# A four-batch WKV and FFN kernel on one core: `w` over ScalarE's queue, eight-column expert masks spread by a product, and another order on all engines

## What is computed

```python
decay = exp(-exp(w)) * (0.5 + 0.5 * tf)
# forward and backward scans  a = a * decay + x  over ek*v (numerator) and ek (denominator)
num = nf + nb - ekv + euk * vf
den = df + db - ek + euk
out = sigmoid(r) * (num / max(den, 1e-8)) * (0.8 + 0.2 * tf)

# layer 0: x = x + experts(WKV(x)): 8 experts of rank 64, one per token by the largest gate
gate = argmax(softmax(xf @ Wg.T)); h = (xf @ A.T) * one_hot(gate); y = h @ Bw.T * 4 * prob
# layer 1: x = x + FFN(WKV(x)): ternary weights made from w1 and w2, 1024 hidden, exact gelu
out = gelu(x @ q(w1).T + b1) @ q(w2).T + b2
```

## Time and profile before

| | |
|---|---|
| median of 3 runs | 103.1 us (101.97, 103.10, 103.27) |
| the profiled execution's own time | 102.21 us |
| its span, first to last instruction | 100.4 us |
| PE busy | 89.8 us, 89% |
| DVE busy | 86.5 us, 86% |
| ACT busy | 79.9 us, 80% |
| POOL busy | 66.3 us, 66% |
| granted TensorE clock, mean | 1.00 |
| HBM read, written | 5.26 MB, 1.05 MB |

### The profile page before, as it was taken

How to read it: one execution, slowest core, us unless ns; L and a number is a source line. 1 busy time by engine, 2 the same in 40 slices (tenths; PEclk the granted TensorE clock), 3 DMA queues, 4 the chain that set the end, 5 groups by cost and what they waited for, 6 DMA issues and landing times. The chain is left out here.

```text
span 100.4 us, 2070 instructions
## 1 busy us (share of the span) xinstructions
PE 89.8 (89%) x633; PEld 80.9 (81%) x633; DVE 86.5 (86%) x203; ACT 79.9 (80%) x144; POOL 66.3 (66%) x90
## 2 busy tenths in 40 slices
PE   3897669989978999999799999999899999799980
PEld 2686549977777888888588888889799999699970
DVE  2479999999999999999999999999999997983330
ACT  4279999999986769999766589997997899976520
POOL 4067679979985697059769897999982967005310
PEclk9999999999999999999999999999999999999999
DMA  1889999700000000000000000000000021100005
GB/s 20 258 262 320 308 245 378 313 3 0 3 0 0 3 0 7 0 0 0 0 3 0 7 0 0 0 0 0 0 0 7 0 104 70 35 0 10 0 0 209
DMA packets 6886, 6.43 MB, mean 64 GB/s; under 512 B 2370, under 2 KB 6492, under 8 KB 6876
## 3 DMA queue, kind: packets, MB, share of 16 engines
q1 hardware_dynamic: 6868, 6.31, 20.1%
q10 hardware_dynamic: 8, 0.00, 0.0%
HBM read 5.26 MB, written 1.05 MB: 63 GB/s over the span
## 5 line engine op out<-in xcount | busy, mean ns | idle before, releaser
L298 POOL TENSOR_TENSOR h_lo<-h,h_hi 128x512 fp32r<-128x512 f32 x9 | 12.3, 1373 | 12.0 <-DVE h_hi L306 7.0
L794 DVE TENSOR_TENSOR_SCAN run<-bank,kv 128x256 f32<-128x256 f32 x32 | 20.0, 670 | 0.1
L1224 PE MATMUL bank<-xin_hi,w1T 128*128 128x256 f32 x64 | 15.8, 287 | 0.9 <-DVE xin_lo L292 0.5
L1156 PE MATMUL bank<-num,AT 128*128 128x256 f32 x64 | 15.5, 384 | 0.7 <-DVE hm L900 0.5
L1258 PE MATMUL bank<-w2T,h_hi 128*128 128x256 f32 x64 | 16.1, 288 | 0.0
L1258 PE MATMUL bank<-w2T,h_lo 128*128 128x256 f32 x64 | 15.6, 281 | 0.0
L611 ACT ACTIVATE h<-bank,bT 128x256 f32<-128x256 f32 x32 | 13.3, 478 | 2.8 <-PE bank L1224 2.6
L1224 PE MATMUL bank<-xin_lo,w1T 128*128 128x256 f32 x64 | 15.2, 278 | 0.0
L1172 PE MATMUL bank<-hm,BT 128*128 128x256 f32 x64 | 14.6, 382 | 0.1
L1224 PEld LDWEIGHTS bank<-xin_hi,w1T 128*128 128x128 f32 x64 | 12.0, 188 | 1.8 <-DVE xin_lo L292 0.8
L1156 PEld LDWEIGHTS bank<-num,AT 128*128 128x128 f32 x64 | 11.6, 190 | 2.2 <-issue 0.9
(11 more groups left out here) (141 smaller groups left out, 216.5 us busy)
## 6 DMA issues: line engine op xcount, KB each, us to landing
w_nat<-in_L_ffn_w_dram SPq DMA_DIRECT2D x2, 1024.0 KB, 8.3
F_nat<-in_fside_BxSxS_dram SPq DMA_DIRECT2D x4, 256.0 KB, 3.5
x_nat<-in_x_dram SPq DMA_DIRECT2D x4, 256.0 KB, 4.9
out_dram<-outb SPq DMA_DIRECT2D x3, 256.0 KB, 2.1
A_nat<-in_L_ffn_A_dram SPq DMA_DIRECT2D x1, 512.0 KB, 5.8
...
wv_rows<-in_L_cond_w_dram SPq DMA_DIRECT2D x2, 1.0 KB
```

Of the source, the lines that this page charges most:

```text
L298: eng.tensor_tensor(h_lo[:, b % 2, 2 * j:2 * j + 2], h32[:, b % 2, 2 * j:2 * j + 2], h_hi[:, b % 2, 2 * j:2 * j + 2].bitcast(F32), ALU.sub ...
L794: dve.tensor_tensor_scan(run[:, r, c, q], decay_ps[:, l, c, b:b + 1].broadcast_to([P, T]), kv[:, b, c, q], 0.0, ALU.mult, ALU.add).then_in ...
L1156: mm = pe.matmul(bank[H_BANK + k][:, (m % 2) * T:(m % 2 + 1) * T], AT[:, c, m * P:(m + 1) * P], num_at(0, b)[:, c], start=(c == 0), stop=( ...
L1224: mm = pe.matmul(bank[g_bank[g]][:, (f % 2) * T:(f % 2 + 1) * T], w1T[:, c, f * P:(f + 1) * P], part[:, b % 2, c], start=(c == 0 and part ...
```

## The change

1. `w` is loaded from ScalarE's queue, and `exp(-exp(w))` is taken on the four rows before the transpose, not after it. VectorE reads the decay's factor from PSUM.
2. An expert mask has 8 columns, one per expert. TensorE transposes it to 8 rows, ScalarE copies these (`copy_hot`), and a product with the constant matrix `spread` (8x128, ones where the partition belongs to the expert) gives the 128 rows (`spread_mask`), which ScalarE copies as before.
3. The reciprocal of the gate's sum leaves `expert_mask` and becomes a call of its own, placed earlier.
4. All four call lists are in a new order, and some calls change engine. To GpSimd go `clip_keys(1)`, `times_tanh(2)` and `(3)`, `h_low(0,3)`, `(1,1)`, `(3,2)`. To VectorE go `seed(0,0,DEN)`, both `seed(1,2)`, `own_values(1,3)`, `add_num(1,2)`, `h_low(1,3)`, `(2,0)`, `(3,1)`, `h_high(1,3)`, `(2,1)`, `(3,2)`, `(3,3)`. To ScalarE go `h_high(2,0)`, `(2,2)`, `(2,3)`.
5. ScalarE has two table loads fewer (ten instead of twelve with the first). TensorE has 21 `keep_warm` transposes instead of 46 and 7 `warm_up` instead of 10.

```diff
-            for k, v in enumerate((w_l0, w_l1)):
-                sp.dma_start(wv_rows[NC * k:NC * (k + 1), :], v.rearrange("(c p) -> c p", p=P)).then_inc(wv_loaded, 16)
...
+            for k, v in enumerate((w_l0, w_l1)):
+                act.dma_start(wv_rows[NC * k:NC * (k + 1), :], v.rearrange("(c p) -> c p", p=P)).then_inc(wv_loaded, 16)
             act.preload_act_table_set("natural_log_exp_and_others")
 
             def decay_exps():
-                act.wait_ge(front_psum, 2)
-                act.activation(edecay[:, :], bank[MISC_BANK][:, VEC_AT:VEC_AT + LAYERS * NC], ACT.Exp).then_inc(edecay_ready, 1)
+                act.wait_ge(wv_loaded, 16 * LAYERS)
+                act.activation(wv_rows[:, :], wv_rows[:, :], ACT.Exp).then_inc(edecay_ready, 1)
                 act.wait_ge(edecay_ready, 1)
-                act.activation(edecay[:, :], edecay[:, :], ACT.Exp, scale=-1.0).then_inc(edecay_ready, 1)
+                act.activation(wv_rows[:, :], wv_rows[:, :], ACT.Exp, scale=-1.0).then_inc(edecay_ready, 1)
...
+            def copy_hot(b):
+                act.wait_ge(hot_psum, b + 1)
+                act.activation(hot_rows[:, b % 2], bank[MISC_BANK][0:NE, MASK_AT:MASK_AT + T], ACT.Copy).then_inc(hot_copied, 1)
...
-            def expert_mask(b):
-
+            def gate_reciprocal(b):
                 both = slice(NT * b, NT * (b + 1))
                 dve.wait_ge(gsum_ready, NT * (b + 1))
                 dve.reciprocal(bank[DVE_BANK][:, GREC_AT + NT * b:GREC_AT + NT * (b + 1)], gsum[:, both]).then_inc(grec_ready, 1)
+
+            def expert_mask(b):
+
...
-                    dve.tensor_scalar(mask[:, i % (2 * NT)], expert_ps, bank[DVE_BANK][:, IDX_AT + i:IDX_AT + i + 1],
+                    dve.tensor_scalar(hot[:, i % (2 * NT)], expert_ps, bank[DVE_BANK][:, IDX_AT + i:IDX_AT + i + 1],
...
-                    mm = pe.transpose(bank[MISC_BANK][:, MASK_AT + n * P:MASK_AT + (n + 1) * P], mask[:, NT * (b % 2) + n], ident[:, :])
-                mm.then_inc(mask_psum, 1)
+                    mm = pe.transpose(bank[MISC_BANK][0:NE, MASK_AT + n * P:MASK_AT + (n + 1) * P], hot[:, NT * (b % 2) + n], ident[:, :])
+                mm.then_inc(hot_psum, 1)
+
+            def spread_mask(b):
+                pe.wait_ge(hot_copied, b + 1)
+                pe.wait_ge(consts_ready, 7 + NE)
+                pe.matmul(bank[MISC_BANK][:, MASK_AT:MASK_AT + T], spread[:, :], hot_rows[:, b % 2], start=True, stop=True).then_inc(mask_psum, 1)
...
             hidden(0, 0)
             hidden(0, 1)
+            expert_in(3, 0)
             transpose_mask(3)
```

More of the change, by code:

```diff
@@ L418, in _ @@
             clip_first_keys(pool, 0)
+            gains()
             clip_first_keys(pool, 1)
-            gains()
             times_values(pool, 0)
             factors()
-            seed(pool, 0, 0, DEN)
-            seed(pool, 0, 1, DEN)
+            clip_keys(pool, 2)
+            clip_keys(pool, 1)
             seed(pool, 0, 0, NUM)
@@ L449, in _ @@
             own_values(pool, 1, 0)
-            add_one(0)
+            own_values(pool, 0, 3)
+            add_num(pool, 0, 3)
             seed(pool, 1, 0, NUM)
-            add_num(pool, 0, 3)
             times_sigmoid(pool, 3)
@@ L455, in _ @@
             num_times_rec(0, 3)
+            add_b2(0)
             add_num(pool, 1, 0)
+            add_one(0)
             times_tanh(pool, 0)
-            add_b2(0)
+            add_one(1)
             num_times_rec(1, 0)
             seed(pool, 1, 1, DEN)
+            seed(pool, 1, 1, NUM)
             add_b2(1)
+            xin_low(pool, 0)
             own_values(pool, 1, 1)
-            add_one(1)
-            xin_low(pool, 0)
-            own_values(pool, 1, 2)
-            seed(pool, 1, 1, NUM)
-            own_values(pool, 1, 3)
             add_num(pool, 1, 1)
             times_tanh(pool, 1)
-            h_low(pool, 0, 0)
-            seed(pool, 1, 2, DEN)
-            add_b2(2)
-            xin_low(pool, 1)
-            h_low(pool, 0, 1)
-            seed(pool, 1, 2, NUM)
-            add_one(2)
+            own_values(pool, 1, 2)
+            xin_low(pool, 1)
+            add_one(2)
+            add_b2(2)
+            h_low(pool, 0, 1)
+            h_low(pool, 0, 0)
             h_low(pool, 0, 2)
-            add_num(pool, 1, 2)
+            h_low(pool, 0, 3)
             h_low(pool, 1, 0)
+            times_tanh(pool, 2)
+            add_b2(3)
+            h_low(pool, 1, 1)
             h_low(pool, 1, 2)
-            h_low(pool, 1, 3)
             add_one(3)
-            h_low(pool, 2, 0)
-            add_b2(3)
-            h_low(pool, 3, 1)
+            times_tanh(pool, 3)
+            h_low(pool, 3, 2)
             h_low(pool, 3, 3)
@@ L627, in _ @@
             sigmoid(3)
+            evacuate_Wg()
             act.preload_act_table_set("natural_log_exp_and_others")
-            key_exp(2)
+            log_den(0, 0)
+            reciprocal(0, 0)
             evacuate_A(0)
@@ L913, in _ @@
             forward_chunk(0, 0, DEN, 0)
+            inverse_gains()
             forward_chunk(0, 0, DEN, 1)
-            clip_keys(dve, 1)
-            inverse_gains()
-            forward(0, 1, DEN)
+            seed(dve, 0, 0, DEN)
+            backward(0, 0, DEN)
+            place_factors()
             forward(0, 0, NUM)
-            place_factors()
-            backward(0, 0, DEN)
             own_keys(0, 0)
             backward(0, 0, NUM)
-            own_keys(0, 1)
+            forward(0, 1, DEN)
             add_den(0, 0)
@@ L985, in _ @@
+            product(1, 1)
+            xin_high(dve, 1)
+            forward(1, 2, DEN)
             select_expert(3, 0)
             select_expert(3, 1)
-            refine_rec(1, 1)
-            forward(1, 2, DEN)
-            product(1, 1)
-            xin_high(dve, 1)
+            seed(dve, 1, 2, DEN)
+            forward(1, 2, NUM)
             backward(1, 2, DEN)
             add_den(1, 2)
-            forward(1, 2, NUM)
+            forward(1, 3, NUM)
+            seed(dve, 1, 2, NUM)
+            own_values(dve, 1, 3)
@@ L994, in _ @@
+            backward(1, 2, NUM)
+            add_num(dve, 1, 2)
             forward(1, 3, DEN)
-            backward(1, 2, NUM)
             den_times_rec(1, 2)
-            forward(1, 3, NUM)
-            times_tanh(dve, 2)
+            refine_rec(1, 2)
             seed(dve, 1, 3, NUM)
             seed(dve, 1, 3, DEN)
-            refine_rec(1, 2)
             product(1, 2)
-            h_low(dve, 0, 3)
-            h_low(dve, 1, 1)
+            backward(1, 3, DEN)
             xin_low(dve, 2)
-            backward(1, 3, DEN)
+            add_den(1, 3)
@@ L1020, in _ @@
+            h_high(dve, 3, 0)
             h_low(dve, 2, 2)
-            h_high(dve, 3, 0)
             h_low(dve, 3, 0)
             h_high(dve, 3, 1)
-            h_low(dve, 3, 2)
-            h_low(dve, 2, 3)
+            h_high(dve, 3, 2)
+            h_low(dve, 3, 1)
+            h_high(dve, 3, 3)
             last_result(dve, 0)
```

289 lines of the change are left out of this document (152 added, 137 removed).

## The result

| | before | after |
|---|---|---|
| median | 103.1 us | 104.06 us (104.01 to 105.19, 5 runs) |
| ratio to the kernel before | | 1.0158, 95% interval 1.0096 to 1.0221 |
| the profiled execution's own time | 102.21 us | 105.19 us |
| its span | 100.4 us | 103.3 us |
| PE, DVE busy | 89.8, 86.5 us | 92.3, 87.1 us |

What follows compares the result with a forecast made beforehand. VectorE was taken to bound until expert_out(2), then TensorE's fixed work. Earlier start -2.0, more work +1.85, fewer waits -1.5 gave -1.65: 100.55 for the profiled execution, median 101.0 us, range 99.4 to 103.2.

Steps and rivals of the forecast that it cites:

- What bounds the kernel: Whole kernel: VectorE sets when layer 1's inputs appear; TensorE must then work off a fixed amount.
- TensorE's fixed work: From expert_out(2) to the last matmul: 41.9 us of work before, 43.75 after the change.
- the sum: From expert_out(2) to the last matmul after the change: 43.75 us of work and 1.1 of waits.
- the small things: On TensorE, four place_output, a mask, a residual and the last transpose_weights: estimated at 2.9 us.
- the waits: TensorE's waits and gaps after expert_out(2): 2.6 of 44.5 us, 1.1 of them left, a gain of 1.5.
- three signs of being wrong: VectorE idle beyond 1 us before 50 us, select_expert waiting for mask_rows, or slow transposes around 15 to 20 us.
- rival (3): Fewer keep_warm: TensorE falls to 1.2 GHz before gate_logits(0), layer 0's first 5.3 us double; 105.5 us; chance 0.06.
- 0.4 us on GpSimd: Delay on times_tanh(2) and (3), also delaying VectorE; part of a rival at 102.2 us, chance 0.20.
- The start: Program start to first scan: new path of w and fewer warm_up gain 0.2 us (bounds 0 and 0.8).
- The masks: On VectorE a mask takes 0.3 us instead of 0.93; three before select_expert(2,1) save 1.9.
- upper bound of 0.5: TensorE's added spread_mask(3) behind expert_out(2): 0.4 us, bounds 0.25 and 0.5.
- The slack of the mask: Between the end of batch 0's mask copy and its use: 1.5 us before, 0.75 in the new order.

Runs made afterwards that it cites:

- e9: Changed kernel with only own_values(1,3) and backward(1,2,NUM) swapped on VectorE: 102.96 us, ratio 1.0069.
- e14: As e11, with 19 and 27 keep_warm in place of 12 and 9: 101.83 us, ratio 0.9874.
- e4: Kernel before, in its old order, with the 8-column masks, copy_hot and spread_mask alone: 109.56 us, ratio 1.0595.
- e11: As e9, with the path of w of the kernel before (SP's queue, exponentials behind the transpose): 102.86 us, ratio 0.9954.
- e3: Kernel before with 12 and 9 keep_warm instead of 19 and 27: 103.74 us, ratio 1.013.
- e8: Kernel before with the new path of w alone: 103.65 us, ratio 1.0118.
- e12: Changed kernel with 20 and 14 keep_warm and eight unread transposes around transpose_mask(0), filling both quiet stretches of TensorE: 103.31 us, ratio 1.0018.
- e6: As e5, with own_values(1,3) called on VectorE behind backward(1,2,NUM): 102.75 us, ratio 0.998.
- e7: As e5, with the 128x128 masks of the kernel before (no copy_hot, no spread_mask): 105.25 us, ratio 1.0199.
- e2: Changed kernel with keep_warm back at 19 and 27 (46 transposes instead of 21): 103.93 us, ratio 1.0121.
- e13: As e12, with own_values(1,3) behind backward(1,2,NUM) and the old path of w: 102.49 us, ratio 0.9881.
- e10: Changed kernel with own_values(1,3) and add_num(1,2) back on GpSimd: 105.54 us, ratio 1.0249.
- e5: Changed kernel with 20 and 14 keep_warm in place of 12 and 9: 104.1 us, ratio 1.0145.

## Why the prediction was wrong

**What bounds the kernel** was read rightly: VectorE until `expert_out(2)`, then TensorE's fixed work. With the collision gone, the second half took 44.5 us in e9 (53.41 to 97.92) and 44.6 in e14; the sum had 44.85. The parts of that sum were less right than their total: TensorE was busy 43.26 of the 44.5 us before, so 1.2 of it was idle, not 2.6. I had set the small things too low, and so overstated both the waits and what could be had from them. Of my three signs of being wrong two came: VectorE was idle for 2.9 us before 50 us (0.8 in the kernel before), and `select_expert` waited 1.73 for `mask_rows`. The third, slow transposes at 15 to 20 us, did not.

**The step that failed first is rival (3), TensorE's clock.** I named the mechanism, gave it 0.06 and argued against it that "the 21 that are left fill 2.4 us, and no gap I find there is over 1 us". There is one of 1.17 us (ahead of `transpose_B(0)`, waiting for `AT`), one of 0.65, and three more from 24 to 27 us, which I had walked through as a delay of the mask and never as idle time of TensorE. I also looked for the fall in the wrong place, ahead of `gate_logits(0)`: in the changed kernel's trace it comes at 27 to 34. (e4's and e11's have one near 15 us as well, e3's and e8's one at 24 to 27.) Its price was too high in turn, 5.3 less 0.75: a short fall costs 1.4 us in e12 (six executions with, six without) and 0.5 to 1.7 in the other kernels that have both, a long one 1.1 more (105.19, one execution, against 104.05). Every execution of the changed kernel had one. The kernel before has them too, in 36 of 66 executions, where a short one costs 0.85. I took the spread of the three times I knew (101.97, 103.10, 103.27) for scatter, and it is about the step between these groups. So the fall doesn't explain by itself why the changed kernel is the slower one: where both have a short fall it is still 1.0 slower (104.05 against 103.05), for the reason that comes next.

**The step that failed second is a term that the sum doesn't have.** `own_values(1,3)` and `add_num(1,2)` move to VectorE, and my sum gives them nothing; at the 0.68 of VectorE's products in the earlier trace rows they would have been 1.3 in all. They took 1.66 and 1.33 from start to start, on the path. The Trainium skill ("SBUF — State Buffer", Reading the diagram) has the rule: a VectorE operation with two SBUF inputs and a GpSimd one that reads SBUF exclude each other for the whole instruction. I cited it and then weighed it as 0.4 us on GpSimd, because the earlier trace rows showed GpSimd's side alone (one `h_low` at 1.67 for 1.28). By that rule the loser is whoever starts second, and beside four `h_low` in a row that is VectorE. The trace agrees, with 1.73 for 0.67. Its price in time at the short fall is 1.1 to 1.3 us (e9, e6), and the tail's 45.8 us for 44.5 is the same 1.3.

**The start.** I took 0.2 us of gain. The decay came at 5.47 as before, and the first scan at 5.89, not 5.69. `w` by ScalarE's queue was there at 4.39, ScalarE's two exponentials took until 5.04, and `transpose_w` waited for them with `transpose_first_F(1)` queued behind it in TensorE's order. I had counted the wait of VectorE and not what stands behind a waiting instruction on TensorE. The term has the wrong sign by 0.2 to 0.6 us in the traces; the times can't tell it apart from none.

**The masks.** Their two products cost 0.41 from start to start, not 0.2 (my estimate 0.1 each; the ceiling was 0.33 each), so a mask saves 0.44, not 0.63, and the three 0.6 less than the 1.9 I took; what the whole edit is worth in this order, e7's four runs leave open. `spread_mask` costs TensorE 0.69, above my upper bound of 0.5. The slack of the mask was right: 0.75 forecast, copied at 27.08 and used at 27.82. It only ran out once TensorE ran at half the rate (e2 and e14, without a fall, have no such wait).

**Together.** From the changed kernel's 104.05: 1.4 for the fall and 1.1 to 1.3 for the collision, if they add, leave 101.4 to 101.6. The executions without a fall that have the swap and the old path of `w` bear that out: 101.19 (e11), 100.96 (e13), 100.88 to 102.04 (e14). The forecast to hold against them is 100.55, that for an execution like the profiled one, which had no fall. The rest, 0.8 to 1.0, is about the masks' 0.6 and the start, where 0.2 of gain became 0.2 of loss; no run splits it. With the two repairs and no fall the order comes near to what I had worked out. What isn't settled is what decides whether an execution has a fall: 2 of 35 without one over the kernels with 21 `keep_warm` (after, e9, e10, e11), 2 of 19 with 34 (e5, e6, e7), 6 of 12 and 1 of 6 with both stretches filled, 4 of 10 and 5 of 6 with 46 (e2, e14). More `keep_warm` in the new order helps on the whole (9 of 16 without a fall against 2 of 35). How often e2 and e14, or e12 and e13, have a fall differs for no reason I can show. The Trainium skill ("TensorE: Matmul & The Clock Gate", What's actually happening) calls the monitor free-running, so that the point of a change varies between runs. The spread within each kernel fits that, and no run here tests it.
